# Projecting q and k of the tile after next in the middle of a step, with the exponentials in front of v

## What is computed

```python
q, k, v = sigmoid(heads(Wq, bq)), sigmoid(heads(Wk, bk)), heads(Wv, bv)
sink_in = normal / einsum(q + EPS, cumsum(k) + EPS)
src_out = normal / einsum(k + EPS, cumsum(q) + EPS)
cons_sink = einsum(q + EPS, cumsum(k * src_out) + EPS) / normal
cons_src = clip(einsum(k + EPS, cumsum(q * sink_in) + EPS) / normal, -1, 1)
e = exp(cons_src); src_comp = e / cumsum(e) * normal
kv = cumsum(k (outer) (v * src_comp))
x = (q * sink_in / normal) . kv * sigmoid(cons_sink)
h = layernorm(inputs + x @ Wo + bo)
y = layernorm(h + gelu(h @ W1 + b1) @ W2 + b2)
x2 = layernorm(inputs + y)
for e in experts:                       # two of eight, by top-k of a softmax
    out += gate_e * (relu(x2 @ wi + bi + (x2 @ A_e) @ B_e) @ wo + bo)
result = layernorm(x2 + out)
```

## Time and profile before

| | us |
|---|---|
| median of 3 runs | 398.22 (398.08 to 398.29) |
| the profiled execution | 396.89 |
| its span, first to last instruction | 395.1 |
| PE busy | 364.5 (92%) |
| PEld busy | 256.9 (65%) |
| DVE busy | 331.0 (84%) |
| ACT busy | 213.9 (54%) |
| POOL busy | 254.5 (64%) |
| the step s = 4, from one first projection to the next | 43.53 |

### The profile page before, as it was taken

How to read it: one execution, slowest core, us unless ns; L and a number is a source line. 1 busy time by engine, 2 the same in 40 slices (tenths; PEclk the granted TensorE clock), 3 DMA queues, 4 the chain that set the end, 5 groups by cost and what they waited for, 6 DMA issues and landing times. The chain is left out here.

```text
span 395.1 us, 6691 instructions
## 1 busy us (share of the span) xinstructions
PE 364.5 (92%) x2050; PEld 256.9 (65%) x2050; DVE 331.0 (84%) x799; ACT 213.9 (54%) x396; POOL 254.5 (64%) x431
## 2 busy tenths in 40 slices
PE   8898989898989999899999999899999998999992
PEld 3565665864749675777567675778477764955652
DVE  3789999979688979998999979997999989844543
ACT  3340418236562896268833885188724874086450
POOL 2043759877499349972898549953898369866231
PEclk9999999999999999999999999999999999999997
DMA  8508055007200029000830047001810054001001
GB/s 252 195 20 195 0 110 159 2 16 171 81 0 2 0 67 229 2 0 2 193 99 2 2 105 189 2 1 28 207 35 1 2 135 105 2 0 29 0 21 33
DMA packets 19875, 26.59 MB, mean 67 GB/s; under 512 B 1664, under 2 KB 9984, under 8 KB 19840
## 3 DMA queue, kind: packets, MB, share of 16 engines
q1 hardware_dynamic: 19696, 25.96, 25.8%
q10 hardware_dynamic: 144, 0.21, 0.2%
HBM read 7.29 MB, written 2.10 MB: 24 GB/s over the span
## 5 line engine op out<-in xcount | busy, mean ns | idle before, releaser
L1036 POOL TENSOR_TENSOR prod<-cum_kv,q_fac 128x512 f32<-128x512 f32 x64 | 93.3, 1474 | 17.3 <-DVE cum_kv L1278 11.8
L458 PEld LDWEIGHTS pO<-s_wor,prod 128*128 128x128 f32 x512 | 63.0, 191 | 19.8 <-issue 11.5
L458 PE MATMUL pO<-s_wor,prod 128*128 128x128 f32 x512 | 67.5, 278 | 4.8 <-POOL prod L1036 4.8
L1272 DVE TENSOR_TENSOR kv<-k,vb 128x512 f32<-128x512 f32 x64 | 53.2, 835 | 1.2 <-DMA vb<-vs 1.2
L1023 POOL TENSOR_TENSOR var_eps<-mv,s_con 128x4 f32<-128x4 f32 x32 | 7.5, 234 | 60.0 <-DVE mv L1300 59.9
L1278 DVE TENSOR_TENSOR_SCAN cum_kv<-p_ones,cum_kv,kv 128x512 f32<-128x512 f32 x32 | 40.6, 1278 | 0.6
L1278 DVE TENSOR_TENSOR_SCAN cum_kv<-p_ones,kv 128x512 f32<-128x512 f32 x32 | 38.8, 1218 | 0.7
L1026 POOL TENSOR_TENSOR rstd<-var_eps,s_con 128x4 f32<-128x4 f32 x32 | 32.9, 1027 | 0.0
L479 PE MATMUL pG<-hT,s_ffn 128*128 128x512 f32 x64 | 31.1, 608 | 1.9 <-ACT hT L860 1.1
L486 PE MATMUL pY<-s_ffn,gel 128*128 128x128 f32 x256 | 32.4, 276 | 0.0
L486 PEld LDWEIGHTS pY<-s_ffn,gel 128*128 128x128 f32 x256 | 30.6, 192 | 1.4 <-issue 0.7
(11 more groups left out here) (199 smaller groups left out, 825.8 us busy)
## 6 DMA issues: line engine op xcount, KB each, us to landing
vb<-vs SPq DMA_DIRECT2D x64, 256.0 KB, 4.6
xT<-x_t SPq DMA_DIRECT2D x8, 256.0 KB, 4.0
xt<-x SPq DMA_DIRECT2D x8, 256.0 KB, 5.2
out<-y SPq DMA_DIRECT2D x7, 256.0 KB, 2.3
s_moe<-moe_w SPq DMA_DIRECT2D x1, 836.0 KB, 9.7
s_wor<-wo_rep SPq DMA_DIRECT2D x1, 512.0 KB, 7.8
s_ffn<-ffn_w SPq DMA_DIRECT2D x1, 512.0 KB, 8.1
s_con<-consts SPq DMA_DIRECT2D x1, 502.0 KB, 4.7
```

Of the source, the lines that this page charges most:

```text
L458: mm = pe.matmul(pO3[:, s, :], prod[:, m % 4, s * P:(s + 1) * P], s_wor[:, m, :], start=False, stop=(m == DH - 1), skip_group_check=True)
L1036: pool.tensor_tensor(prod[:, m % 4, :], cum_kv[t.par][:, m, :], q_fac[t.par][:, :], ALU.mult).then_inc(prod_ready, 1)
L1272: dve.tensor_tensor(kv[:, m % 3, :], k[t.par][:, :], vb[:, m, :], ALU.mult).then_inc(kv_ready, 1)
```

## The change

`n` is a new name, tile s+2. In a steady step:
- TensorE: `project_q` and `project_k` are those of n and stand behind `reduce_out(b, 2)`; `third_step` has those of tile 3 at its end. The head sums of a stand directly behind `reduce_out(b, 7)`, `project_v(a)` behind them, and then the first three `expert_out`.
- ScalarE: `q_out(n)` and `k_out(n)` behind `x2T_out(c)`; `gate_exp(c)` in front of `v_out(a)`.
- VectorE: `cumulate_q(n)` in front of `values(a)` and `cumulate_k(n)` behind `join_moments(d, 3)`; the sums of tile 3 alone stay at the front of step 2.
- SyncE: `load_xT(n)` at the front of the list, for n from 4 on.
- The waits follow the banks' new order of users: `project_v(a)` waits for `q_out(n)`, the first head sum of a for `k_out(n)`.
- `third_step`: `ffn_out(b, 0..3)` in one piece; on VectorE `cumulate_kv(a, 3)` in front of `moments(b, 1)`, an outer product and its sum behind it; on GpSimd `product(a, 2)` in front of `inverse_std(b, 1)`; on ScalarE `seed_x(a)` and `udT_out(c)` in front of the `relu`s. In step 2 `product(b, 3)` stands in front of `inverse_std(c, 2)`.

No arithmetic changes.

```diff
@@ SyncE, step
+                if A and a.plus(1).exists() and a.n >= 3: load_xT(a.plus(1))
                 if B: spread_vs(b, 4); spread_vs(b, 5); spread_vs(b, 6)
                 if A and a.n >= 2: load_xt(a)
                 if B: spread_vs(b, 7)
-                if A and a.plus(1).exists() and a.n >= 2: load_xT(a.plus(1))
+                if A and a.n == 2: load_xT(a.plus(1))
@@ TensorE, project_q / project_k / project_v / head_sums
-                elif t.n > 2:
+                elif t.n == 3:
                     pe.wait_ge(qfac_ready, t.n)
-                if t.n == 3:
                     pe.wait_ge(hsum_ready, 1)
+                elif t.n > 3:
+                    pe.wait_ge(qfac_ready, t.n - 1)
+                    pe.wait_ge(q_ready, t.n)
...
+                elif t.n > 3:
+                    pe.wait_ge(vs_ready, t.n - 1)
+                    pe.wait_ge(k_ready, t.n)
...
-                elif t.n > 2:
-                    pe.wait_ge(q_ready, t.n + 1)
+                elif 2 < t.n < TILES - 1:
+                    pe.wait_ge(q_ready, t.n + 2)
+                elif t.n == TILES - 1:
+                    pe.wait_ge(qfac_ready, t.n)
...
+                    if pair == 0 and 2 < t.n < TILES - 1:
+                        pe.wait_ge(k_ready, t.n + 2)
+                    elif pair == 0 and t.n == TILES - 1:
+                        pe.wait_ge(vs_ready, t.n)
@@ TensorE, third_step
-                ffn_out(b, 0)
+                for f in range(FC):
+                    ffn_out(b, f)
+                u_T(c, False)
                 inter1(c, 0); inter1(c, 1)
-                ffn_out(b, 1)
-                u_T(c, False)
-                ffn_out(b, 2); ffn_out(b, 3)
+                reduce_out(a, 0)
                 inter2(c, 0); inter2(c, 1)
-                reduce_out(a, 0)
+                project_q(a.plus(1)); project_k(a.plus(1))
@@ TensorE, step
-                if A: project_q(a); project_k(a)
+                n = a.plus(1)
                 if D: inter_base(d, 2); inter1(d, 2); inter_base(d, 3); inter1(d, 3)
                 if B: reduce_out(b, 1)
                 if D: inter2(d, 2); inter2(d, 3)
                 if B: reduce_out(b, 2)
+                if n.exists(): project_q(n); project_k(n)
                 if C: x2_T(c)
                 if B: reduce_out(b, 3); reduce_out(b, 4)
                 if C: logits_and_lora(c)
                 if B: reduce_out(b, 5); reduce_out(b, 6); reduce_out(b, 7)
-                if D: expert_out(d, 0)
-                if A: project_v(a); head_sums(a, 0, True); head_sums(a, 0, False)
-                if D: expert_out(d, 1); expert_out(d, 2)
+                if A: head_sums(a, 0, True); head_sums(a, 0, False); project_v(a)
+                if D: expert_out(d, 0); expert_out(d, 1); expert_out(d, 2)
@@ ScalarE, third_step
+                seed_x(a); udT_out(c)
                 relu(c, 0); relu(c, 1)
-                udT_out(c); seed_x(a)
+                normalise(b, 1)
                 gated_constant(c)
-                normalise(b, 1)
+                q_out(a.plus(1)); k_out(a.plus(1))
@@ ScalarE, step
-                if A: q_out(a); k_out(a)
+                n = a.plus(1)
                 if D: relu(d, 2); relu(d, 3)
                 if C: normalise(c, 2); x2T_out(c)
+                if n.exists(): q_out(n); k_out(n)
+                if C: gate_exp(c)
                 if A: v_out(a)
-                if C: gate_exp(c)
@@ GpSimd, third_step and step
-                inverse_std(b, 1); product(a, 2); scaled_n2(b)
+                product(a, 2)
+                inverse_std(b, 1); scaled_n2(b)
...
+                elif B: product(b, 3)
...
-                if B: product(b, 3); product(b, 4); product(b, 5); product(b, 6); product(b, 7)
+                if B and b.n > 2: product(b, 3)
+                if B: product(b, 4); product(b, 5); product(b, 6); product(b, 7)
@@ VectorE, third_step
-                outer_product(a, 2); cumulate_kv(a, 2); outer_product(a, 3)
+                outer_product(a, 2); cumulate_kv(a, 2); outer_product(a, 3); cumulate_kv(a, 3)
                 moments(b, 1)
+                outer_product(a, 4); cumulate_kv(a, 4)
                 second_relu(c, 0); second_relu(c, 1)
-                cumulate_kv(a, 3); outer_product(a, 4)
-                cumulate_kv(a, 4)
+                outer_product(a, 5)
                 moments(b, 2)
-                outer_product(a, 5)
@@ VectorE, step
-                if A: cumulate_q(a); cumulate_k(a)
+                if A and a.n == 3: cumulate_q(a); cumulate_k(a)
...
+                n = a.plus(1)
                 if D: piece_moments(d, 3)
+                if n.exists(): cumulate_q(n)
                 if A: values(a)
                 if D: join_moments(d, 3)
+                if n.exists(): cumulate_k(n)
                 if B: moments(b, 1)
```

## The result

| | before | after |
|---|---|---|
| median, same chip | 398.15 (397.95 to 398.29) | 392.77 (392.64 to 393.37) |
| ratio, 95% interval | | 0.9868 (0.9851 to 0.9885) |
| the profiled execution | 396.89 | 392.84 |
| its span | 395.1 | 391.1 |

The change is 5.4 us faster by the medians and 4.05 us by the two profiled executions.

What follows compares the result with a forecast made beforehand. No engine is full; a chain passes between VectorE, GpSimd and TensorE. Step 2 -0.4, steps 3 to 5 3 x -0.64, step 6 -1.15 sum to -3.5 us: 398.22 becomes 394.7 us, range 393.0 to 397.2.

Steps and rivals of the forecast that it cites:

- slower case through `k_out(n)`: New chain `outer_product(b, 7)`, `k_out(n)`, first head sum of a, with 2.6 us of cover; if late, 400.3 us; chance 0.07.
- (3): TensorE's q and k projections of n, 1.72 us, move behind `reduce_out(b, 2)`; new wait about 1.3 us; costed at nothing.
- (5): SyncE's load of xT(n) ahead of spreads 4 to 7: costed at nothing, 0 to 1 us per step kept for the range.
- the first rival: More gain: outer products' 0.35 us wait for spread 3 shrinks, 0.2 to 0.4 us in four steps; 393.2 us; chance 0.14.
- term (2): VectorE from `sink` to `outer_product(a, 0)`: running sums add 2.36 us, filled waits give 1.85; 15.57 becomes 16.08 us, +0.51.
- -0.64: Net forecast per steady step, 3 to 5: 16.08 - 15.57 - 1.15 us, the 1.15 being `sink` starting sooner.
- term (7): Step 6 has no n, so no projection or running sum, and keeps the whole 1.15 us gained at `sink`.
- Term (4): ScalarE: q and k sigmoids of n behind `x2T_out(c)` fit its 7.27 us wait; `gate_exp` before v costs nothing.
- Term (6): Third step's reordering and step 2: the extra projections leave little of the 1.76 us wait; -0.4 us, bounds -1.0 and +0.5.
- The rule against the change: VectorE with two SBUF inputs and GpSimd reading SBUF exclude each other; both addition groups slow would give 395.9 us; not expected.

## Why the prediction was right, and where it failed

**Right: the mechanism and its signs.** The waits that it named are there or gone as said: VectorE waits 1.22 us in front of `sink` (forecast 1.2) and not at the values or the moments; TensorE doesn't wait at the head sums, and has a new wait at `reduce_out(b, 1)` (0.78 us, forecast 1.3); steps 3 to 5 take 42.4 to 42.95 us (42.9). TensorE's part in front of `sink` was forecast as 6.3 us and is 6.32. The slower case through `k_out(n)` has not come about: k is out at 207.0 and the head sum starts at 209.60, the 2.6 us of cover as worked out. Of the parts costed at nothing, (3) and (5) held: TensorE still waits 0.32 us for the last product, and the place of the load makes no measurable difference. The 1.3 us in (3) came from a wrong time, which the sum doesn't use: without its 1.72 us of projections TensorE would reach `reduce_out(b, 1)`, which starts at 243.45 us in the kernel before, at 243.45 - 1.72 = 241.73 us and not at 241.2, and the wait would be 1.1.

The time lies near that of the first rival (393.2), but not by its mechanism: the outer products 2 and 3 still take 1.67 us together (1.68 before), and GpSimd still waits 0.27 us in front of `product(7)` (0.26).

**How far off it was.** The median fell by 5.45 us from 398.22, where 3.47 was forecast. Of the 1.98 us more, 0.90 lie in the stretches of the table and 1.08 outside them, in how the medians stand to the profiled executions. Either alone would have left the time inside the range (393.8 and 393.7).

**The first step that failed: term (2), from `sink` to `outer_product(a, 0)`.** The forecast was 15.57 + 2.36 - 1.85 = 16.08 us for every step; step 4 has 231.33 - 215.57 = 15.76. Both sizes in it were off.

- The sums. They were priced at the spacing of the earlier trace rows, 1.18 us each. In step 4 of the changed kernel they are those of tile 6, the first of a batch entry, whose sum needs no carry: 227.50 - 226.38 = 1.12 and 229.48 - 228.38 = 1.10, together 2.22.
- The waits. What they gave is what the stretch would have grown by without them, less what it grew by: 15.57 + 2.22 - 15.76 = 2.03 us, where the brackets say 0.86 + 0.80 + 0.19 = 1.85. In step 3 the sums (tile 5, with a carry; the starts are 183.67 and 184.85, 185.73 and 186.90) take 1.18 + 1.17 = 2.35 and the stretch went from 15.50 to 15.60: the waits gave 2.25, their brackets in the kernel before say 1.02 + 0.80 + 0.23 = 2.05. These are VectorE's rows of that kernel in step 3, and under them those of the changed one:

```profile
174.48 0.68 DVE L1210 TENSOR_TENSOR q_sink<-q,pA 128x512 f32<-128x512 f32 x1
...
186.08 0.69 DVE L1267 TENSOR_TENSOR vs<-v,pB 128x512 f32<-128x512 f32 x1 [1.02 <-PE pB L406]
...
187.87 0.89 DVE L1290 BATCH_NORM_STATS2 stats<-pY 128x6 f32<-128x128 f32 x4 [0.80 <-PE pY L486]
...
189.98 0.69 DVE L1272 TENSOR_TENSOR kv<-k,vb 128x512 f32<-128x512 f32 x1 [0.23 <-DMA vb<-vs]
```

```profile
173.11 0.69 DVE L1226 TENSOR_TENSOR q_sink<-q,pA 128x512 f32<-128x512 f32 x1 [1.21 <-PE pA L417]
...
188.71 0.69 DVE L1288 TENSOR_TENSOR kv<-k,vb 128x512 f32<-128x512 f32 x1
```

So three waits gave 0.18 to 0.20 us more than their brackets. Part of the reason is in the rows of the changed kernel: VectorE's `stats` at 225.59 lasts 0.86 us, but the sum behind it starts 0.79 us after it, 0.07 us before its end; behind a wait there is no such overlap, and the bracket counts only from the end. And one step's waits stood for all three steps. The term is +0.19 in step 4 and +0.10 in steps 3 and 5 (step 5: from 277.18 - 261.71 = 15.47 to 274.08 - 258.51 = 15.57), not +0.51. Less the 0.10 by which `sink` gained less than forecast (1.06 in place of 1.15 in step 4: the transpose took 0.64 us to reach `sink`, not 0.54), this is the 0.2 to 0.3 us by which steps 3 to 5 beat -0.64, together 0.86 us. The whole stretch beat the sum by 0.90; steps 2 and 6, 0.21 better and 0.17 worse than forecast, nearly cancel.

**The second step that failed: the median from the span.** The prediction carried the 1.3 us between the profiled execution and the median of the kernel before over to the changed kernel. That distance was gone: the profiled executions differ by 4.05 us, and the changed kernel's profiled execution, 392.84, lies 0.07 us above its median, where that of the kernel before lay 1.33 us below. 4.05 + 1.33 + 0.07 = 5.45. Against these 1.40 us stands the opening of the changed kernel's profiled execution, 0.29 us longer than that of the other. What the runs show of the reason is this: the profiles differ in front of the first `sink` by up to 1.2 us, and of 54 later executions of the kernel before only 8 took 397.95 us or more, as all four of the first comparison did. So that median lay high. Beside the later runs of the kernel before the changed one gained 3.9 us. Why those four were slow stays open.

**A smaller miss: term (7).** Step 6 has no sums to take in and keeps what `sink` gains: 1.05 us measured at the `sink`, 0.98 at the end, 1.15 forecast. It is the same 0.1 us as above.

**Term (4) was right in its number and missed what the move is for.** It put the exponential in front of v at nothing, "it waits for VectorE either way". It does, and v loses nothing. But with the sums gone from the front the old place, behind v, would cost 2.5 us. The forecast came out because the change has it in the right order, which is luck: nothing in the working asked what the load of 1.28 us would stand behind once VectorE comes 2.36 us sooner.

**Term (6)**, -0.4 for step 2, measured -0.61. That it is so near is partly luck: `sink` came 0.60 us sooner where 0.8 to 1.0 was forecast, and the stretch from `sink` to `outer_product(a, 0)` grew by 0.00 us (15.88 both times) where 0.51 was. The reason to count it low held: the third step's edit alone gives 1.6 us, and nearly all of that pays for the two projections.

**The rule against the change.** The prediction named the Trainium skill, "SBUF — State Buffer", section "Who interferes with whom", by which both groups of GpSimd's additions might become slow, and expected them only to change places. GpSimd of the changed kernel (beside the earlier trace rows):

```profile
251.46 2.60 POOL L1062 TENSOR_TENSOR x_b2n<-xt,s_row 128x128 f32<-128x128 f32 x4
254.02 1.69 POOL L1097 TENSOR_TENSOR x2c<-x,c_gate 128x128 f32<-128x128 f32 x4
```

VectorE beside it:

```profile
251.37 0.69 DVE L1200 SCALAR_TENSOR_TENSOR kq<-k,cum_q 128x512 f32<-128x512 f32 x1
...
252.07 0.84 DVE L1208 SCALAR_TENSOR_TENSOR qk<-q,cum_k 128x512 f32<-128x512 f32 x1
```

The first group is now the slow one, 2.60 us in place of 1.70, and the second the fast one, 1.69 in place of 2.60. The 0.9 us are paid once, as before, and the rule's estimate of 395.9 has not come about. The rows agree with the rule as such: the slow group is the one that runs beside `kq` and `qk`, which read both inputs from SBUF.

## What to carry to other kernels

Where engines take turns at the limit, moves come in sets. Of the three moves here, the head sums first cost 11.5 us alone, the exponential in front of v is worth nothing alone, and both without the sums' move cost 6 us (403.44 beside 397.36). The sums' move with only one partner keeps 1.3 us (without the head sums) or 1.8 us (without the exponential) of the rigid stretch's 4.3; the sums' move alone was not run. Price a move only after asking which order on the other engines had its cover from the moved work. Before moving an activation on ScalarE, find the table load that goes with it or with its new neighbour: a load is free where the engine waits for data behind it and costs its 1.28 us where it stands behind that wait.

## What the runs showed that I had not expected

- A wait of 1.96 us of TensorE was followed in four steps of two kernels by some 3 us at a granted clock of 1.2 GHz, half of full speed, at 1.5 to 1.8 us a time, and in four others, with the same wait, by none. What decides between them no run here shows. The changed kernel has 1.00 in every window from 60 to 360 us.
- The first projection of the program, two matmuls, takes 1.10 us in some executions and up to 2.08 us in others (the third step alone), while the clock column shows 1.00. The time in front of the first `sink` varies with it, so that effects below 1 us are better read from there on.
- Three waits gave a little more when they were filled than their brackets said: 1.85 us of brackets gave 2.03 us, and 2.05 gave 2.25.
